# DPP attention: the products with the token's own key and the weighting of the values go from VectorE to GpSimd

## The reference

```python
sim = where(arange(Tn) <= i, k @ q_i, -inf)
_, top_idx = top_k(sim, 8)                       # 8 slots
for comb in COMBS:                               # 8 single slots, 28 pairs
    idx = concat([i, top_idx[comb]])
    K, V = k[idx], v[idx]
    gram = einsum('cnd,cmd->cnm', K, K)
    score = log(det(gram) + 1e-6) / (s + 1)
    w = softmax(einsum('cnd,d->cn', K, q_i) / HS ** 0.5)
    out = einsum('cn,cnd->cd', w, V)
y = softmax(scores) @ outs          # v[i] where no combination is valid
```

## Time and profile before

| | |
|---|---|
| median of 3 runs | 6926.5 us (6921.05 to 6927.41) |
| the profiled execution's own time | 6929.71 us |
| its span, first to last instruction | 6928.0 us |
| the `l2a` stage, 1485 to 4605 us | DVE busy 2895.56 of 3120.00 us, PE 2331.67, ACT 1603.19, POOL 173.52 |

### The profile page before, as it was taken

One profiled execution on the slowest core, in us unless ns is written; L12 is line 12 of the kernel. 1 busy time (PEld: TensorE's weight loads), 2 busy tenths in 40 slices (PEclk: granted clock), 3 DMA queues, 4 the chain that ended last, 5 costly groups with the idle time before them and its releaser, 6 DMA issues. The chain is left out here.

```text
span 6928.0 us, 139785 instructions
## 1 busy us (share of the span) xinstructions
PE 4892.4 (71%) x46024; PEld 3814.4 (55%) x46025; DVE 4586.2 (66%) x10128; ACT 2648.7 (38%) x8929; POOL 1447.6 (21%) x1237
## 2 busy tenths in 40 slices
PE   6777777967777777777777777751794397169990
PEld 2333335756656666666666566551583376169990
DVE  5777773249999999999999999952464444212223
ACT  3334332225555455554554555532220132223330
POOL 2332331110000000000000000005325300554447
PEclk8777778977676777667776676655897697589995
DMA  4000000011111111111111111111222102111113
GB/s 139 7 5 7 7 0 6 0 38 69 69 65 68 69 69 69 69 69 67 69 72 63 69 69 69 69 39 53 72 76 72 41 0 60 51 53 46 45 42 109
DMA packets 139932, 369.61 MB, mean 53 GB/s; under 512 B 29410, under 2 KB 94667, under 8 KB 113716
## 3 DMA queue, kind: packets, MB, share of 16 engines
q1 hardware_dynamic: 105556, 283.58, 11.8%
q0 software_dynamic: 33792, 78.69, 3.6%
HBM read 286.69 MB, written 75.50 MB: 52 GB/s over the span
## 5 line engine op out<-in xcount | busy, mean ns | idle before, releaser
L2660 PE MATMUL l2a_g<-l2a_feat,l2a_onehot 128*128 128x33 bf16 x27648 | 780.9, 183 | 403.7 <-ACT l2a_values L2263 202.1
L2660 PEld LDWEIGHTS l2a_g<-l2a_feat,l2a_onehot 128*128 128x128 bf16 x27648 | 765.3, 100 | 473.6 <-issue 237.3
L2526 DVE TENSOR_REDUCE l2a_dots<-l2a_prod 128x144 f32<-128x2304 f32 x192 | 489.6, 2550 | 4.5
L2609 PE MATMUL l2a_s<-l2a_qkT 32*128 32x128 f32 (+1 forms) x1536 | 486.1, 452 | 0.0
L1892 PE MATMUL l_y<-l_hc,l_selT 128*96 128x512 f32 x384 | 300.2, 876 | 262.2 <-POOL l_hc L1730 261.7
L2632 PE MATMUL l2a_m<-main_ident,l2a_pv 128*96 128x128 f32 x2304 | 335.2, 317 | 152.2 <-DVEq L2467 152.2
L2632 PEld LDWEIGHTS l2a_m<-main_ident,l2a_pv 128*96 128x96 f32 x2304 | 327.2, 199 | 172.3 <-issue 168.8
L1730 POOL TENSOR_TENSOR l_hc<-l_hs,l_bc 128x512 f32<-128x512 f32 x192 | 243.4, 1268 | 717.3 <-DVE l_hs L1797 716.1
L2534 DVE TENSOR_SCALAR l2a_onehot<-l2a_spread,l2a_pos 128x4096 bf16<-128x4096 bf16 x288 | 360.7, 1281 | 43.8 <-DVE l2a_hd L2428 20.1
L2609 PEld LDWEIGHTS l2a_s<-l2a_qkT 32*128 32x128 f32 x1536 | 310.6, 250 | 85.6 <-issue 37.9
L700 PE MATMUL l3f_expert_h<-l3f_tT,l3f_w_own 96*128 96x256 f32 x2592 | 333.6, 287 | 8.9 <-POOL l3f_w_own L657 6.7
(11 more groups left out here) (412 smaller groups left out, 11365.5 us busy)
## 6 DMA issues: line engine op xcount, KB each, us to landing
l2a_spread<-l2a_idx_rows SPq DMA_DIRECT2D x192, 1024.0 KB
rows_in<-main_zeros SPq DMA_DIRECT2D x1, 13824.0 KB, 59.6
l2f_xg<-rows_in SPq DMA_DIRECT2D x72, 192.0 KB, 2.4
rows_out<-l2f_ys POOLq DMA_DIRECT2D x72, 192.0 KB, 2.4
l3f_xg<-rows_in SPq DMA_DIRECT2D x72, 192.0 KB, 2.4
rows_out<-l3f_ys POOLq DMA_DIRECT2D x72, 192.0 KB, 2.4
l3f_w<-in_l3f_w SPq DMA_DIRECT2D x2, 4608.0 KB, 32.8
l_xT<-in_l_xT SPq DMA_DIRECT2D x16, 384.0 KB, 3.7
```

The source lines that it names most:

```text
L2526: nc.vector.tensor_reduce(dots[:, quad_of(s[2]), 0:NPROD], prod[:, :, :, :], AX.X, ALU.add).then_inc(S["dots_ready"], 1)
L2609: ins = nc.tensor.matmul(o, qkT[rows, u, j, t * P:(t + 1) * P], qkT[rows, u, 4 + j // 2, 0:nk], start=False, stop=j % 2 == 1, skip_group_c ...
L2660: ins = nc.tensor.matmul(o[:, a * FEAT:a * FEAT + 2 * HS + 1], onehot[:, kt, at:at + P], feat3[:, s[1], kt, part, h, 0:2 * HS + 1], start= ...
```

## The change

What it does:

1. `products` keeps the gram products in `prod`. The cross products move to a GpSimd function `cross_products`, which writes a new two-deep buffer `cross_prod`. `sums` becomes two reductions, one over `prod` and one over `cross_prod`; the second waits for `cross_ready`.
2. `weigh_stage` no longer multiplies the values with `alpha`. GpSimd does it in `weigh_values`, three instructions of four heads each, at OUT, one step later. `values` has four buffers (two images times two tiles).
3. GpSimd's waits for `prod_ready` become a wait for `calm` in every step. `calm` is a bare increment that VectorE's program has at the head of `sums`, ahead of its wait for `prod_ready`.
4. On TensorE `turn_output` moves from WEIGH to OUT, ahead of the front matmuls. `project` moves between the second and the third head of the gather. On ScalarE `turned` moves ahead of `bend`. On VectorE `add_out` moves to the end of the step, behind `sums`.

```diff
+        values = m.sb("values", [P, 4, H, SLOTS, HS + 1])
+        prod = m.sb("prod", [P, QUAD, NPROD - SLOTS, HS])
+        cross_prod = m.sb("cross_prod", [P, 2, QUAD, SLOTS, HS])
...
+                def weigh_values(n, u, t):
+                    r = n * 2 + t
+                    pool.wait_ge(S["alpha_ready"], counted(r + 1))
+                    pool.wait_ge(S["yT_psum"], counted(r))
+                    for h in range(0, H, 4):
+                        ins = nc.gpsimd.tensor_tensor(
+                            pv[:, 0:SLOTS, h * HS:(h + 4) * HS].rearrange("p a (h d) -> p h a d", h=4),
+                            values[:, 2 * u + t, h:h + 4, :, 0:HS],
+                            alpha[:, h:h + 4, :].unsqueeze(3).broadcast_to([P, 4, SLOTS, HS]), ALU.mult)
+                    ins.then_inc(S["pv_ready"], 1)
+
+                def cross_products(s):
+                    q, t = count_of(s), s[2] // QUADS
+                    pool.wait_ge(S["kv_ready"], counted(q * QUAD + QUAD))
...
+                    nc.gpsimd.tensor_tensor(cross_prod[:, s[2] % 2, :, :, :], keys[:, s[2] % 2, :, 0:SLOTS, :],
+                                            mine.unsqueeze(2).broadcast_to([P, QUAD, SLOTS, HS]), ALU.mult
+                                            ).then_inc(S["cross_ready"], 1)
...
-                    if s and ((nxt and i == 4) or (i < 2 and in_range(n))):
-                        pool.wait_ge(S["prod_ready"], count_of(s) + 1)
+                    if back(3):
+                        pool.wait_ge(S["calm"], count_of(back(3)) + 1)
                         hold(pool, S["pool_held"])
+                    if stage(back, OUT):
+                        weigh_values(*stage(back, OUT))
...
-                    link(TT(pv[:, 0:SLOTS, :].rearrange("p a (h d) -> p h a d", h=H), values[:, t, :, :, 0:HS],
-                            alpha[:, :, :].unsqueeze(3).broadcast_to([P, H, SLOTS, HS]), ALU.mult))
...
-                    nc.vector.tensor_tensor(prod[:, :, 0:SLOTS, :], key[:, :, 0:SLOTS, :],
-                                            mine.unsqueeze(2).broadcast_to([P, QUAD, SLOTS, HS]), ALU.mult
-                                            ).then_inc(S["prod_ready"], 1)
...
                 def sums(s):
                     q = count_of(s)
+                    dve.sem_inc(S["calm"], 1)
                     dve.wait_ge(S["prod_ready"], q + 1)
-                    nc.vector.tensor_reduce(dots[:, quad_of(s[2]), 0:NPROD], prod[:, :, :, :], AX.X, ALU.add
-                                            ).then_inc(S["dots_ready"], 1)
+                    nc.vector.tensor_reduce(dots[:, quad_of(s[2]), SLOTS:NPROD], prod[:, :, :, :], AX.X, ALU.add)
+                    dve.wait_ge(S["cross_ready"], counted(q + 1))
+                    nc.vector.tensor_reduce(dots[:, quad_of(s[2]), 0:SLOTS], cross_prod[:, s[2] % 2, :, :, :], AX.X,
+                                            ALU.add).then_inc(S["dots_ready"], 1)
```

62 lines of the change are left out of this document (33 added, 29 removed).

## The result

The changed kernel takes 7191.4 us (median of 4 runs, 7187.90 to 7195.53) against 6926.95 us before, a ratio of 1.0384 with an interval of 1.0366 to 1.0402. That is 264.5 us, 8.3 us per image. The forecast was 6985 us with a range of 6858 to 7065 us: the sign was right, the size was not, and the time lies outside the range.

A forecast was written before the change was run, and what follows sets the result against it. VectorE was taken as the bound, busy 90.25 of 95.66 us per image. Per image -6.7 + 0.5 + 2.2 + 3.8 + 2.0 = +1.8 us, times 32 +58 us: median 6985 us, 8-in-10 range 6858 to 7065 us.

The forecast's parts named there:

- What VectorE is rid of: VectorE per image: cross products 3.60 us and weighting 3.58 us go, the second reduction adds 0.5 us; 6.7 us less.
- `calm` does not put GpSimd under the reduction: GpSimd's start: calm rises before or at the start of compare, 4 to 5 us ahead of the reduction.
- The shared port: VectorE and GpSimd exclude each other; a GpSimd instruction fully in the way costs VectorE 0.95 us, at most 1.08 us.
- The rival that VectorE keeps the port: VectorE's gapless instructions hold the port, so weighting waits for the reduction and costs 0; 6862 us, chance 0.30.
- Weighting: GpSimd's weighting in steps 1 and 4: four of six instructions delay VectorE, 3.8 us per image, bounds 0 and 5.7 us.
- Cross products: GpSimd's six cross products per image delay VectorE's two-input instructions by 2.0 us, bounds 0 and 4.3 us.
- I take half for the other four: Cross products outside steps 2 and 5: half the possible delay assumed, 2.0 us per image.
- What becomes late: Step 2: add_out on VectorE waits for project on TensorE; step lasts 17.2 to 18.2 us instead of 15.27, +2.2 us.
- everything in the way: Rival: all port delays at their upper bounds and step 2's wait at +3.2 us; +7.0 us per image, 7150 us, chance 0.12.
- the wait and the saving lost in it: Step 2: +2.2 us for add_out's wait for project, and 0.5 us of VectorE's saving that goes into that wait.

The follow-up runs named there:

- Run 6: Kernel before with only the cross products moved to GpSimd, started behind prod_ready, under the first of two reductions; 6846.3 us, ratio 0.9885.
- run 2: Changed kernel with GpSimd waiting for the end of the products (prod_ready) instead of calm; 7054.1 us, ratio 1.0185.
- runs 6 and 7: Kernel before with only the cross products moved to GpSimd: started behind prod_ready, 6846.3 us; started as soon as the keys are there, 6973.2 us.
- run 5: Changed kernel with GpSimd waiting for prod_ready instead of calm and doing the cross products only then, ahead of its other jobs; 6909.4 us, ratio 0.9976.
- run 4: Changed kernel with bend put ahead of turned on ScalarE; 7153.5 us, ratio 1.0324.
- Run 8: Kernel before with only the moves on TensorE, ScalarE and VectorE and the four value buffers; products and weighting stay on VectorE; 7110.2 us, ratio 1.0276.
- Run 1: Changed kernel with GpSimd's weighting and cross product instructions cut to 16 of 512 elements each, waits and orders kept; 6894.3 us, ratio 0.9952.

## Why the prediction failed, by its own steps

**What VectorE is rid of (6.7 us): right, as far as runs show it.** The first reduction takes 2017 ns and the second 676 ns, and starts overlap by 0.08 us; the two cost 2.61 us where the one cost 2.55 us. Run 6 gained 78 us and gave 20 us away at the loop's end, together 98 of the 102 us that its expectation has for the cross products by the same prices. The weighting's 3.6 us have no run of their own.

**`calm` does not put GpSimd under the reduction: right.** It rose at the comparison's start (GpSimd starts at 3105.82, the comparison at 3105.73), 6.9 us ahead of the reduction, and run 2 gave back 4.3 us per image.

**The shared port: right in kind.** The rival that VectorE keeps the port is false. With both queued they alternate, so every weighting instruction that meets a comparison or a product costs about 0.86 us, where the forecast took 0.95 us. The Trainium skill (SBUF — State Buffer, section Who interferes with whom) says that issue order and not the operation's shape decides who blocks, and that a tensor_reduce never contends; both agree with the rows here: the first comparison of step 4, issued before GpSimd's instruction, keeps its 1.27 us and GpSimd waits, and the reductions keep 2017 ns.

**Weighting, 3.8 us: right in the main**, 4.3 us measured (run 2). Five of the six instructions are in the way, three in step 4 and two in step 1, and not four.

**Cross products, 2.0 us: mis-sized, by half.** Measured 4.0 us (runs 6 and 7) and 4.5 us (run 5, of which 1.1 us lie in step 2, where TensorE's clock has its part), near the upper bound of 4.3 us. The step that failed is the choice ("I take half for the other four"): they do not fall under find but behind it, on L2521 to L2476 of the weigh stage in steps 1 and 4 and on the comparison in steps 0 and 3. The place of one instruction was read from a trace in which the gather stood elsewhere, and for the rest half was taken where the upper end was as near.

**What becomes late, +2.2 us: the step that failed most.** The length of step 2 was within the sum (17.2 to 18.2 us forecast, 18.18 us in the mean), but by terms that erred against each other. TensorE had stood still for 2.51 us ahead of `turn_indices`, and it and the scores took 4.52 us instead of 2.70 us, at a mean granted clock of 0.56, so largely at the lower level of 1.2 GHz. The windows of the changed kernel show it, and the front units at full clock afterwards. The last line is the front of the kernel before, from which the forecast took its 5.78 us: it ran at 0.52.

```profile
3167.28:3171.80 4.52, 4.52 (x11) 2.44 (x11) 4.11 (x14) 0.52 (x3) 0.00 (x0) 0.56 0.01 2
3171.80:3177.20 5.40, 5.40 (x37) 5.40 (x37) 4.18 (x5) 0.00 (x0) 0.00 (x0) 0.73 0.37 120
3177.20:3182.34 5.14, 5.14 (x73) 4.05 (x72) 3.08 (x3) 4.94 (x20) 0.00 (x0) 1.00 0.21 81
...
3043.85:3049.63 5.78, 5.78 (x13) 3.49 (x12) 5.51 (x9) 4.36 (x16) 0.00 (x0) 0.52 0.44 156
```

`turn_output` took 5.57 us instead of 4.09 us, the front 3.0 us instead of 4.7 to 5.8 us. The forecast had added up durations from stretches of different clock: slow for the front and `project`, fast for the rest. That step 2's length came out inside its range is therefore luck. With all pieces at full clock there is no wait at all (run 5, the first of the two images). That a gap ahead of the scores lowers the clock stood only as an argument of the rival "everything in the way", and had no term of its own. The order of `turned` and `bend` on ScalarE was in the diff and was overlooked; by run 4 it moves the wait and costs 1.2 us per image, outside step 2. The large error is that the term ended with step 2. Run 8 measured 5.8 us per image for the moves, where the sum had 2.7 us (the wait and the saving lost in it): 2.8 us of it lie in steps 0, 1, 4 and 5: in the gather and the logarithms, which come later, in small jobs of GpSimd that now meet VectorE, and in the loop's end, which no longer hides under a reduction.

**The sum with measured terms:** -6.7 + 5.8 (run 8) + 4.3 (run 2) + 4.5 (run 5) = 7.9 us against 8.3 us measured. The rest is not assigned, and the terms are not independent: TensorE's clock, and with it step 2, changes with the others. Run 1 fits the first two: -6.7 + 5.8 = -0.9 us, and tiny_pool came out 1.1 us per image below the kernel before. The rival "everything in the way" (7150 us, chance 0.12) was nearest and still 41 us short; its wait, too, was one step's alone.

## What to carry to other kernels

Work given to GpSimd beside VectorE costs or gains by its starting time: put it under VectorE's reductions, by a wait on an instruction that has ended and not by a bare increment, which rises as early as the sequencer gets there. A step that is moved on a chain of three engines must be followed until every engine is back in its old place, and not just to the first wait. When durations from a trace are added up for a new order, look at the granted clock of each, and put a price on the idle time that the new order opens on TensorE. Wherever a wait stands near a loop's end, look whether it lays the branch open.
